# Moving GpSimd's table products and weight sums behind the first feed-forward input, and two slot groups into the experts' steps

## What is computed

```python
gate = jax.nn.softmax(tok @ Wgate.T, axis=-1)
k_cap = bs // E
vals, idx = jax.lax.top_k(gate.T, k_cap)
idx_flat = idx.T.reshape(-1)
w = vals.T
g = _ln(tok[idx_flat], mlp_g, mlp_b).reshape(k_cap, E, d)
y = jnp.einsum('ked,ehd->keh', g, fc1s) + b1s
y = jax.nn.gelu(y, approximate=True)
y = jnp.einsum('keh,edh->ked', y, fc2s) + b2s
y = y * w[..., None]
tok = tok.at[idx_flat].add(y.reshape(-1, d))
```

## Time and profile before

| | us |
|---|---|
| median of three runs | 2720.74 |
| lowest and highest | 2714.67, 2722.98 |
| the profiled execution | 2719.1 |
| its span in the trace | 2716.9 |
| TensorE busy in the span | 2491.5 (92%) |
| VectorE busy | 1742.9 (64%) |
| ScalarE busy | 1191.5 (44%) |
| GpSimd busy | 495.9 (18%) |
| first expert's first product, from the start of the span | 1045.27 |
| layer 2's first feed-forward product | 1891.08 |

### The profile page before, as it was taken

One profiled execution on the slowest core, in us unless ns is written; L12 is line 12 of the kernel. 1 busy time (PEld: TensorE's weight loads), 2 busy tenths in 40 slices (PEclk: granted clock), 3 DMA queues, 4 the chain that ended last, 5 costly groups with the idle time before them and its releaser, 6 DMA issues.

```text
span 2716.9 us, 63322 instructions
## 1 busy us (share of the span) xinstructions
PE 2491.5 (92%) x25441; PEld 1941.4 (71%) x25441; DVE 1742.9 (64%) x3876; ACT 1191.5 (44%) x2456; POOL 495.9 (18%) x472
## 2 busy tenths in 40 slices
PE   6998799999999847997999999996999699879999
PEld 5876466666666636886888888885666587668888
DVE  5888778888887675553554555445555498955554
ACT  5886455555555502341333323332333477623322
POOL 1333001001001115553110111011000265500000
PEclk9999899999999958998999999997999899989999
DMA  6000000000000042454000000000000133200000
GB/s 214 3 3 2 20 23 31 23 23 31 23 23 31 13 134 84 116 138 131 12 0 0 0 0 0 0 1 1 1 1 0 40 111 111 94 8 8 16 16 16
DMA packets 72144, 102.21 MB, mean 38 GB/s; under 512 B 10864, under 2 KB 50288, under 8 KB 71472
## 3 DMA queue, kind: packets, MB, share of 16 engines
q1 hardware_dynamic: 65840, 91.46, 10.5%
q0 software_dynamic: 6144, 8.56, 1.7%
HBM read 67.20 MB, written 32.80 MB: 37 GB/s over the span
## 4 chain that ended last, share of the span: by engine, by line
PE 79%; DMA 7%; DVE 6%; issue 2%; ACT 2%; POOL 2%; SPq 1%; DVEq 0%; POOLq 0%; ACTq 0%
PE psW L322 17%; PE psW L315 9%; PE psP L1405 8%; PE psS L1540 8%; DMA rotated<-work 6%; PE psP L437 4%; PE psP L430 4%; PE psS L1532 4%; PE psO L1405 4%; PE psW L529 3%; PE psS L381 3%; PE psO L414 3%; PE psO L346 2%; PE psP L397 2%; PE psW L1405 2%
## 5 line engine op out<-in xcount | busy, mean ns | idle before, releaser
L322 PE MATMUL psW<-r,work 128*128 128x512 f32 x1024 | 481.7, 604 | 1.0 <-DVE work L773 1.0
L1270 POOL TENSOR_TENSOR work<-work 128x512 f32<-128x512 f32 x128 | 132.0, 1042 | 1135.4 <-DVE work L807 1135.3
L322 PEld LDWEIGHTS psW<-r,work 128*128 128x128 f32 x1024 | 181.0, 191 | 162.1 <-issue 156.5
L315 PE MATMUL psW<-work,r 128*128 128x128 f32 x2048 | 243.5, 278 | 1.0 <-DVE work L773 1.0
L315 PEld LDWEIGHTS psW<-work,r 128*128 128x128 f32 x2048 | 234.8, 193 | 3.5 <-DVE work L773 1.4
L1540 PE MATMUL psS<-r,work 128*128 128x256 f32 x992 | 216.8, 380 | 0.4 <-ACT slots L2311 0.4
L1405 PE MATMUL psP<-work,r 128*128 128x256 f32 x768 | 191.8, 387 | 17.2 <-DVE work L1615 16.5
L1540 PEld LDWEIGHTS psS<-r,work 128*128 128x128 f32 x992 | 188.5, 191 | 25.2 <-ACT slots L2311 0.5
L1184 ACT ACTIVATE work<-work 128x512 f32<-128x512 f32 x128 | 80.1, 626 | 276.5 <-DVE work L786 276.5
L1785 ACT ACTIVATE work<-psP 128x512 f32<-128x512 f32 x64 | 38.2, 597 | 362.5 <-PE psP L1405 362.5
L1405 PEld LDWEIGHTS psP<-work,r 128*128 128x128 f32 x768 | 148.2, 194 | 41.7 <-issue 10.6
(11 more groups left out here) (309 smaller groups left out, 5070.4 us busy)
## 6 DMA issues: line engine op xcount, KB each, us to landing
r<-in_l_fc SPq DMA_DIRECT2D x16, 1024.0 KB, 6.6
rotated<-work SPq DMA_DIRECT2D x60, 256.0 KB
work<-mod_rows SPq DMA_DIRECT2D x64, 128.0 KB, 2.8
work<-rotated SPq DMA_DIRECT2D x30, 256.0 KB
r<-in_l_w SPq DMA_DIRECT2D x2, 3072.0 KB, 14.5
x<-in_x SPq DMA_DIRECT2D x8, 512.0 KB, 9.8
gather_table<-work SPq DMA_DIRECT2D x32, 128.0 KB, 1.8
moe_sum<-work SPq DMA_DIRECT2D x32, 128.0 KB, 1.7
```

The source lines that it names most:

```text
L315: ins = nc.tensor.matmul(ps[:, q * P:(q + 1) * P], w[:, k, lo + q * P:lo + (q + 1) * P], L.hT[:, k, :], start=(k == 0), stop=(k == KC - 1))
L322: ins = nc.tensor.matmul(ps[:, 0:width], L.hT[:, k, :], w[:, k, lo:lo + width], start=(k == 0), stop=(k == KC - 1))
L1270: nc.gpsimd.tensor_tensor(E, E, halves(L.rs)[i].unsqueeze(2).broadcast_to([P, 8, N]), ALU.mult).then_inc(L.s[f"prob{i}"].sem, 1)
```

## The change

- GpSimd: table product 2 leaves its place ahead of gather 1, table product 3 its place behind it. A wait for the first `f_h` is put behind gather 1. Products 2 and 3 now open steps 0 and 1, each ahead of that step's weight sums.
- VectorE: the tables of group 2 and the first of group 3 are no longer made ahead of the first normalisation; both tables of group 2 open step 0, both of group 3 open step 1. The normalisation of step 1 has its usual place behind c11(0) again. In `norm`, the copy of the gate column goes from the start to the end, and carries the signal.
- TensorE: groups 2 and 3 are summed in `result` of steps 0 and 1, behind block r = 2, and turned behind block r = 3. Their places in PSUM are psP's two halves. Before B(1) of steps 1 and 2 it waits for the slots. The transposes of step 1 take their usual places in `hidden`.
- ScalarE: the copies of groups 2 and 3 stand at the end of steps 0 and 1.
- Layer 3's weight sums wait for layer 2's first `f_h`.

```diff
@@ pe_ff @@
-                early = ahead and not (Q.kind == "moe" and t == 0)
+                early = ahead
...
                 B(0)
+                if Q.kind == "moe" and 0 < t < 3:
+                    pe.wait_ge(rt["slots"], t + 2)
                 B(1)
...
+                    if r == 2 and late_group:
+                        pe_slot_sums(pe, late_group)
                 ins.then_inc(Q.s["f_y"].sem, 1)
...
-                late_slots = Q.kind == "moe" and t == 0
-                if late_slots:
-                    pe.wait_ge(rt["slots"], 3)
+                late_group = t + 2 if Q.kind == "moe" and t < 2 else 0
                 hidden(t, u, ahead)
-                if late_slots:
-                    pe_slot_sums(pe, 3)
-                    after(pe, *Q.summed(0, "c11", M - 1))
-                    turn(1, 0)
-                    turn(1, 1)
-                    pe_slot_turn(pe, 3)
-                    pe.wait_ge(rt["slots"], len(GROUPS))
-                result(t, u)
+                result(t, u, late_group)
+                if late_group:
+                    pe_slot_turn(pe, late_group)
...
-            if Q.kind == "moe":
-                pe_slot_sums(pe, 2)
-                pe_slot_turn(pe, 2)
@@ dve_ff, norm @@
-                    after(v, Q.s["f_done"], n - 1)
-                    nc.vector.tensor_copy(Q.wcol[u].unsqueeze(2), Q.xg[u][:, :, n + D:n + D + 1])
...
+                if Q.kind == "moe":
+                    ch.link(ins)
+                    after(v, Q.s["f_done"], n - 1)
+                    ins = nc.vector.tensor_copy(Q.wcol[u].unsqueeze(2), Q.xg[u][:, :, n + D:n + D + 1])
                 ins.then_inc(Q.s["f_xn"].sem, 1)
@@ dve_ff, hidden_two and start @@
-                late = Q.kind == "moe" and t == 0
-                if late:
-                    dve_hot_b(3)
+                if Q.kind == "moe" and t < 2:
+                    dve_hot_a(2 + t)
+                    dve_hot_b(2 + t)
                 c11(t, 0)
-                if ahead and not late:
+                if ahead:
                     norm(t + 1, (t + 1) % 2)
...
-                if late:
-                    norm(1, 1)
...
-            else:
-                dve_hot_a(2)
-                dve_hot_b(2)
-                dve_hot_a(3)
@@ act_ff @@
-                if Q.kind == "moe" and t == 0:
-                    act_slots(a, 2)
...
-                if Q.kind == "moe" and t == 0:
-                    act_slots(a, 3)
+                if Q.kind == "moe" and t < 2:
+                    act_slots(a, 2 + t)
@@ pool_moe @@
             pool_hot(g, 1)
-            pool_hot(g, 2)
             gather(1)
-            pool_hot(g, 3)
+            after(g, Q.s["f_h"], 1)
             for t in range(NG):
+                if t < 2:
+                    pool_hot(g, 2 + t)
@@ slots @@
-        SLOT_SUMS = [psP[:, 0:512], psP[:, 512:1024], psS[:, 0:256], psS[:, 512:768]]
-        SLOT_TURNS = [psO[:, 0:512], psO[:, 512:1024], psS[:, 256:512], psS[:, 768:1024]]
+        SLOT_SUMS = [psP[:, 0:512], psP[:, 512:1024], psP[:, 0:512], psP[:, 0:512]]
+        SLOT_TURNS = [psO[:, 0:512], psO[:, 512:1024], psP[:, 512:1024], psP[:, 512:1024]]
@@ gpsimd program @@
             following(g, "l2")
+            after(g, Q["l2"].s["f_h"], 1)
             g.wait_ge(ld["l3"], 80)
             pool_weight_sums(g, Q["l3"], 0, 0)
```

More of the change, by code:

```diff
@@ L1525, in chunks, with result @@
                         yield 2 * m + j
-            def result(t, u):
+            def result(t, u, late_group=0):
                 after(pe, Q.s["f_done"], t)
```

## The result

| | before | after |
|---|---|---|
| median, us (6 runs each, one chip) | 2719.64 | 2706.36 |
| lowest and highest | 2714.67, 7461.07 | 2702.28, 2710.5 |
| ratio, 95% interval | | 0.9949 [0.9934, 0.9964] |
| span of the profiled execution | 2716.9 | 2708.7 |

A forecast was written before the change was run, and what follows sets the result against it. TensorE was taken to wait for VectorE, held by GpSimd on one shared way into SBUF. Terms -9.2 - 2.65 + 1.4 + 1.6 + 1.9 - 7.6 gave -14.5 us: 2720.7 to 2706.2 us, range 2697 to 2717.

The forecast's parts named there:

- Part 1: Gather 0 of the first expert: without VectorE's three tables beside it, its issues end 2.2 us sooner.
- Rival (a): Gather 0: its stretch has another cause, so the gathers don't gain; -12.3 us in all, 2708.4 us, chance 0.07.
- Part 2: First normalisation and group 1: TensorE's order sets the eight transposes, which start at 1030.6 instead of 1033.72, -3.1 us.
- Part 3: Chain to the first product: L1613 to L1615 without GpSimd, -6.1 us; gather 1 beside them 0, bound 0 to 1.
- Part 4: Experts' step 0: group 3's work goes, early transposes return, -2.65 us; result(0) gains group 2's sums and turn, +1.4.
- 1.5 of slow clock at the start: Experts' step 0: 1.5 us of its 4.3 over a later step, put down to the lower clock in the old profile.
- Part 5: Experts' step 1: VectorE's tables ahead of c11(0) delay F(0), +1.6 us; result(1) gains group 3's sums and turn, +1.9.
- Part 6: Layer 2's feed-forward: VectorE's held Newton instructions are freed, -7.6 us; only the next normalisation meets the moved sums, 0, bound 1.
- The queues: GpSimd's and SyncE's queues: the later scatter, gather and weight loads cost nothing.
- Rival (b): GpSimd holds the normalisation too: +2.6 us in step 0, +1 in layer 2, 0.5 in step 1; 2710.3 us, chance 0.15.
- (c): Step 1: VectorE's tables wait behind one or two scatter issues and the clock restarts low; +7 us, 2713 us, chance 0.12.
- (d): Steps 0 and 1: GpSimd goes first each time, so VectorE's tables and normalisations wait; +25 us, 2731 us, chance 0.03.

The follow-up runs named there:

- one wait alone: The kernel before with one added line: GpSimd waits for the first f_h behind gather 1, ahead of table product 3; 2715.43 us, 0.998.

## Why the prediction was right, and where it was not

- **The bound** (VectorE held by GpSimd, TensorE waiting) was read rightly: the held instructions are at their medians, and one wait alone moved the first product by 6.07 us. An instruction that waits isn't always served next: L1613's 4.61 us in before (1037.76 to 1042.37) cover two instructions of GpSimd, which end at 1040.86 and 1042.07.
- **Part 1, gather 0:** last issue's end 5.21 us after the first issue's start (forecast 5.17). Rival (a) fell with group 2's tables put back.
- **Part 2:** transposes 9.71 us after gather 0's start (forecast 9.84), set by TensorE's order.
- **Part 3:** the chain lost all of its 6.1; nothing of the bound of 1 for the gather beside it was used.
- **Part 4, step 0:** mis-sized by +1.0 us. The failed term is "1.5 of slow clock at the start", taken over from before. The low clock lasted 5.2 us instead of 2.8; free of it and of the hold, the step is 13.06. The miss could have been anything from 0.5 to 1.5, for the same instructions took 15.14 to 16.10 us in other profiles. Result(0)'s 1.4 was 1.47.
- **Part 5, step 1:** 1.65, of which 1.55 by the mechanism named, VectorE's queue. The term that was late is the normalisation ahead of the turn, not c22(0). Result(1)'s 1.9 was 2.07.
- **Part 6:** the -7.6 stood; its "0, bound 1" for the next normalisation was +0.87, inside its bound. The low clock was 1.5 us longer than in before, half of which is 0.7; the hold alone would have kept the step at 15.66 as well.
- **The queues:** nobody waited for the scatter or for the later gathers.
- **Rival (b)** named a mechanism that is real: four normalisations took 4.40 and 4.82 us. I gave it 0.15 as a case that excludes the forecast, but it cost nothing in step 0 of the changed kernel's two profiles, since the low clock gave the slack that it used up. Its price of +2.6 was too high as well: 0.6 where the low clock was short, 1.3 with the clock up. Its +1 for layer 2 measured 0.1 to 0.4 beside the low clock and 2.15 with the clock up. **Rivals (c) and (d)** had VectorE wait behind the scatter; it was the scatter that waited.
- **The sum** was 2.0 us too large by the stretches. The runs' 13.9 (9.8 to 18.0 by the interval) can't tell -14.5 from -12.55, so the near hit of the median (2706.36 against 2706.2) is in part luck. The low clock's length is one piece of that luck.

## What to carry to other kernels

Where GpSimd has tensor work that nobody needs soon, put it behind the signal on which the matmul engine starts, but behind the next normalisation too, not just the first input. (Alone, that second move gave nothing here that runs can tell, 0.9949 for layer 2; it pays once the clock is up.) A wait that is removed ahead of a phase leaves the clock to come up inside the phase: size that term apart, and don't take its length over from the old profile. Two causes that lie beside each other show nothing when one is taken away; take both away.

## What was not expected of the hardware

- A VectorE TENSOR_SCALAR with one SBUF input and two pointer scalars is held by GpSimd's TENSOR_TENSOR: 1.75 us for four becomes 4.37 to 6.80.
- A VectorE TENSOR_TENSOR of two f16 inputs in SBUF stretches indirect DMA issues, gathers from 0.95 to 2.79 and scatters from 1.64 to 2.90 us.
- In the same instructions of the experts' step 0 the clock stayed at 0.50 for 2.9 us in two profiles (step 0 15.14), for 5.2 and 5.5 in two others (15.63, 15.75) and for 6.2 in a fifth (16.10). The idle time ahead doesn't order them: it was 3.5 us in all five, and 7.2 in before, with 2.8 us of low clock. In the two of 2.9 us and in that of 6.2 the clock had risen to 1.00 by the end of the first transposes and fell again before the first product. What decides the length stays open. With transposes up to the first product, the clock was at 1.00 from that product on in all three such profiles.
